# Graph-attention pair stage: normalising four row tiles on ScalarE instead of VectorE

## The reference, cut to what matters

```python
score = s_src + s_dst + einsum(diff, a_dif) + einsum(abs(diff), a_abs) + einsum(hr_src*hr_dst, a_prd)
alpha = leaky_relu(score, negative_slope=0.2)          # one per head and edge: 8 x 10000
ex    = exp(alpha - segment_max(alpha)[src])
att   = ex / (segment_sum(ex, src)[src] + 1e-16)
gnn   = segment_sum(att[:, :, None] * h_e[:, dst], src)
...
x = x + gnn + mix                    # mix: linear attention on the same input
x = x + ffn(_layernorm(x, axis=-1))  # (x - mean) / sqrt(var + 1e-5), over the 512 features
```

## Time and profile before

| | us |
|---|---|
| median of three runs | 1072.98 (1068.33 to 1073.06) |
| the profiled execution, whole | 1073.43 |
| its span, first to last instruction | 1071.6 |
| PE / DVE / ACT / POOL busy in the span | 979.7 / 759.3 / 338.8 / 349.8 |
| TensorE's mean granted clock | 0.967 of 2.4 GHz |

### The profile page before, as it was taken

The page is one execution under the profiler, slowest core; times in us unless marked ns, Lnnn a source line. Parts: engine busy times, 40 slices in busy tenths (PEclk is TensorE's granted clock), DMA queues, the critical chain, the costliest instruction groups (busy, mean ns, idle before and its releaser), DMA issues.

```text
span 1071.6 us, 12287 instructions
## 1 busy us (share of the span) xinstructions
PE 979.7 (91%) x4324; PEld 648.0 (60%) x4324; DVE 759.3 (71%) x1309; ACT 338.8 (32%) x623; POOL 349.8 (33%) x316
## 2 busy tenths in 40 slices
PE   7899999999999979998896899999988859888998
PEld 6874696544494445744454447776666527777864
DVE  8897697343794666845445768998877759999643
ACT  5874473322402213022114122321213304444511
POOL 2006731000300102011010147777777714555500
PEclk9999999999999989999898899999998978999999
DMA  9999120113300114001130244333343287531101
GB/s 308 293 301 293 50 99 1 54 45 117 99 29 1 42 57 146 1 0 56 50 118 0 83 122 122 98 91 100 100 137 93 80 329 292 205 133 56 49 1 48
DMA packets 66093, 115.14 MB, mean 107 GB/s; under 512 B 11517, under 2 KB 43517, under 8 KB 64501
## 3 DMA queue, kind: packets, MB, share of 16 engines
q1 hardware_dynamic: 57077, 93.10, 25.8%
q0 software_dynamic: 8960, 21.31, 7.2%
HBM read 85.91 MB, written 28.49 MB: 107 GB/s over the span
## 4 chain that ended last, share of the span: by engine, by line
PE 40%; DVE 28%; POOL 14%; issue 8%; DMA 7%; ACT 1%; SPq 0%; POOLq 0%; DVEq 0%; ACTq 0%
PE ps L752 16%; PE ps L890 7%; POOL arena L685 6%; DMA pairs<-arena,pairi 5%; DVE arena L1620 5%; POOL pairs L695 4%; DVE arena L1977 4%; PE ps L761 4%; PE ps L795 3%; PE ps L744 3%; DVE arena L1962 2%; DVE arena L1986 2%; PE ps L944 2%; PE ps L1111 2%; POOL small L644 1%
## 5 line engine op out<-in xcount | busy, mean ns | idle before, releaser
L752 PE MATMUL ps<-arena 128*125 128x512 f32 x400 | 180.5, 607 | 1.0 <-DVE xn L1654 1.0
L621 POOL TENSOR_TENSOR small<-small 125x1 f32<-125x1 f32 x50 | 35.0, 699 | 389.8 <-DVE small L1433 389.8
L752 PEld LDWEIGHTS ps<-arena 128*125 128x125 f32 x400 | 75.6, 194 | 91.0 <-issue 89.8
L752 PE MATMUL ps<-arena,xnT 128*125 128x512 f32 x240 | 108.7, 610 | 5.0 <-DVE x L1886 4.2
L1266 ACT ACTIVATE arena<-ps,cols 128x125 f32<-128x125 f32 x120 | 43.2, 466 | 201.9 <-PE ps L744 201.9
L977 PE MATMUL ps<-ex_low,high 125*125 125x512 f32 x400 | 104.2, 406 | 0.0
L695 POOL DMA_INDIRECT pairs<-arena,pairi x80 | 87.2, 1090 | 27.1 <-issue 24.7
L744 PE MATMUL ps<-ident,arena 125*125 125x125 f32 (+3 forms) x425 | 62.4, 283 | 25.9 <-ACT arena L1123 10.0
L719 POOL TENSOR_TENSOR arena<-arena,counts 125x625 f32<-125x625 f32 x40 | 57.5, 1438 | 78.5 <-ACT arena L1387 35.5
L752 PEld LDWEIGHTS ps<-arena,xnT 128*125 128x125 f32 x240 | 46.0, 194 | 60.9 <-issue 59.5
L744 PEld LDWEIGHTS ps<-ident,arena 125*125 125x125 f32 (+3 forms) x425 | 53.5, 168 | 47.7 <-issue 19.4
(11 more groups left out here) (222 smaller groups left out, 1872.1 us busy)
## 6 DMA issues: line engine op xcount, KB each, us to landing
pairs<-fill SPq DMA_DIRECT2D x10, 2500.0 KB, 22.3
arena<-in_mw SPq DMA_DIRECT2D x6, 2048.0 KB, 8.3
arena<-pairs SPq DMA_DIRECT2D x4, 2500.0 KB, 14.2
arena<-pairs SPq DMA_DIRECT2D x8, 1250.0 KB, 6.1
arena<-pairs SPq DMA_DIRECT2D x8, 625.0 KB, 7.6
arena<-in_qkv_w SPq DMA_DIRECT2D x1, 3072.0 KB
arena<-in_cw SPq DMA_DIRECT2D x3, 1024.0 KB, 5.3
arena<-in_w_qkvT SPq DMA_DIRECT2D x1, 3072.0 KB
```

Source lines behind the costliest of these rows:

```text
L752: last = mm(slot[0:m, lo:hi], lhsT_of(k), rhs_of(k)[:, lo:hi], start=(k == 0), stop=(k == ks - 1))
```

## The change

For tiles 0 to 3 the 125x512 instruction leaves DVE. DVE now computes only `shift = -mean * rstd` (125x1, a `scalar_tensor_tensor`) at the same place in its loop and signals a new semaphore `shift_ready`; it waits for `rstd_ready` there, as `ln_apply` did. ACT waits for `shift_ready` and makes the tile as `Identity(rstd * x + shift)`, one 125x512 activation, which then signals `xn_ready`. In ACT's loop this stands in the same step (17, 25, 33, 41) behind the `Exp` and ahead of the four short activations. Tile 4 stays on DVE. `shift` lies in a part of the tile `small` that was free.

```diff
+        shift = small[0:P, 192:192 + NT]
 ...
                     act.activation(Sg, Sg, ACT.Exp, scale=-1.0,
                                    bias=smax[:, 1, h:h + 1]).then_inc(sig("pair_exp"), 1)
+                j, left = divmod(g - LAG - SUM_LAG - NORM_LAG, H)
+                if 0 <= j < NT - 1 and left == H - 1:
+                    act.wait_ge(sig("shift_ready"), j + 1)
+                    act.activation(xn[:, j, :], x[:, j, :], ACT.Identity, scale=rstd[:, j:j + 1],
+                                   bias=shift[:, j:j + 1]).then_inc(sig("xn_ready"), 1)
                 j, h = divmod(g - LAG - SUM_LAG, H)
 ...
                 j, left = divmod(g - LAG - SUM_LAG - NORM_LAG, H)
-                if 0 <= j < NT and left == H - 1:
+                if 0 <= j < NT - 1 and left == H - 1:
+                    lns_done[0] += 1
+                    v.wait_ge(sig("rstd_ready"), lns_done[0])
+                    STT(out=shift[:, j:j + 1], in0=mv[:, j, 0:1], scalar=-1.0, in1=rstd[:, j:j + 1],
+                        op0=ALU.mult, op1=ALU.mult).then_inc(sig("shift_ready"), 1)
+                if j == NT - 1 and left == H - 1:
                     normed_x(j)
```

## The result

| | before | after |
|---|---|---|
| median, us | 1072.97 (1066.86 to 1075.91, 12 runs) | 1080.34 (1074.11 to 1087.19, 12 runs) |
| ratio | | 1.0075, 95% interval 1.0050 to 1.0101 |
| profiled execution / its span | 1073.43 / 1071.6 | 1083.11 / 1081.3 |
| mean granted clock in it | 0.967 | 0.957 |

The changed kernel is slower, by 7.4 us in the median, where 1075.6 was forecast.

The account below looks back on a forecast made before the run. DVE was taken to pace the pair stage for four tiles, PE for the last; -0.56 + 1.34 + 0.47 + 1.4 = +2.65 on 1073.43 gave 1076.08, so 1075.6 us for the median, range 1070.0 to 1079.0.

Parts of the forecast that it names:

- The shift is held: On DVE, the shift ends only with POOL's product, so DVE gains 0.28 us per tile, 0.56 for tiles 0 and 1.
- ScalarE's price: On ACT, the 125x512 activation takes 0.80 us, 0.70 until the next instruction may start.
- The late copies: ACT's copies of exT come 2.07 us late in steps 17 and 25 without loss; step 33 loses 1.34 us.
- The tail: Step 41, at the stage's end: PE's transpose comes later, a loss of 0.47 us, bounds 0 and 0.7.
- TensorE's clock: Behind PE's longer pauses in steps 17 and 25 the clock falls once to 1.2 GHz, costing 1.4 us.
- part 3: The prediction's step on TensorE's clock in steps 17 and 25: one fall expected, 1.4 us.
- Rival (d): Steps 17 and 25: clock low for 12.6 us after a pause, 4.3 us per tile; +9.9, 1082.4; chance 0.08.
- (c): The shift issues ahead of POOL's product and takes 0.16 us; DVE gains 3.1 us; -2.2, 1070.8; chance 0.11.
- (e): PE's delays are won back everywhere and DVE keeps its gain; -0.56, 1072.4; chance 0.07.

Follow-up runs that it names:

- e2: The changed kernel with the shift made by a tensor_scalar with one SBUF input instead of a two-input scalar_tensor_tensor; ratio 1.0015 to the kernel before.
- e5: The changed kernel with POOL's products of steps 16, 24 and 32 starting only when the shift is done; ratio 1.0014 to the kernel before.
- e10: The kernel before, with POOL's products of steps 16, 24 and 32 starting only when VectorE's normalisation of the tile is done; ratio 0.9988.
- e1: The changed kernel with 12, 12 and 7 spare TensorE products filling the pauses of steps 17, 25 and 33; 1074.39 us, ratio 1.0014.
- e8: The changed kernel with only tiles 0 and 1 normalised on ScalarE, the others on VectorE; ratio 1.0057 to the kernel before.
- e7: The changed kernel with only tile 2 normalised on ScalarE, the others on VectorE; ratio 1.0026 to the kernel before.
- e6: The changed kernel with ScalarE's activation cut to 8 of 512 columns, its wait kept; median 1080.27 us, ratio 1.0073 to the kernel before.

## Why the prediction was wrong, point by point

- **The shift is held: right.** 1.46 us were measured where about 1.4 was forecast, ending with POOL's product, and VectorE gained 0.27 us per tile (0.28). Shown by e2 and e5, and by e10 for the instruction that the shift replaces.
- **ScalarE's price: right.** 0.81 us for 0.80.
- **The late copies: right.** TensorE's pauses were 2.94 and 3.16 us, as worked out, and 1.76 in step 33 (a delay of 1.66 on a gap of some 0.1). The tail lost 0.50 (0.47). What all this costs at full clock was put at +1.25; e1 measures 1.5 in the medians and 1.35 in its stage from step 17 on, with +1.33 in step 33 where 1.34 was forecast.
- **TensorE's clock: wrong, and that is the whole error.** The step that failed is part 3. It put the clock at one fall of 1.4 us in the two pauses of steps 17 and 25 and at nothing in step 33, for which it gives no reason. Between e1 and after, which differ in the filled pauses alone, the clock cost 7.4 - 1.5 = 5.9 us in the medians and 11.69 - 1.35 = 10.3 in the profiled executions, with three falls. Two things were mis-sized. First, which pauses count: the two rows of 2.71 us in the earlier trace rows came from an earlier stage, and the prediction took them as the edge between falling and holding. In this stage the clock fell behind pauses of 1.61, 1.67, 1.75, 1.76, 1.82 and 1.89 us, all there were of that length. Second, how long it stays low: 2.7 us up to one step were assumed, 3.4 to 10.5 were measured. The trace of before held a row against both that was not used, a pause of 2.01 us behind which the clock fell and stayed low for 6.7 us (timeline, busy time by stretch):

```profile
610.81 1.09 PE L744 MATMUL ps<-ident,xn 125*128 125x125 f32 x4 [2.01 <-DVE xn L1441]
...
610.80:617.50 6.70, 5.89 (x13) 3.25 (x14) 6.46 (x21) 1.18 (x2) 0.99 (x2) 0.50 0.97 399
```

- **Rival (d) had the mechanism, at 0.08.** It priced 12.6 us at half speed at 4.3 us per tile and found only tiles 0 and 1 in danger; with falls of about 10 us e8 shows 3.1 per tile, and tile 2 adds 4.7 (e7), 1.3 of which the forecast had as lateness. Its time should read 1082.8: 1.25 + 8.6 on 1072.98, not the 1082.4 that stands there. The row that it rested on, 12.6 us at 0.50 with TensorE busy throughout, was the better guide, because it came from this very stage with the same instructions; it was set aside for a row of another stage.
- **The chances.** 0.15 were given to slower by more than 0.5%. The forecast's own reading, that pauses of 0.9 to 1.1 us would grow to 3, should have moved more weight there.
- **(c) and (e)** didn't come: the shift came second in all three steps of the stage, and the delays weren't won back.

What stays open: why the changed kernel's executions spread from 1074 to 1087 us. Their mean granted clocks go along: 0.965 in those of 1074.1 and 1075.9 us, 0.953 in that of 1087.2. So the number and length of falls differ from run to run, but only one execution was profiled, and why a pause of 2.52 us was followed by none (e6) and one of 1.61 by one (e5) isn't known. Nor is why the stage's part ahead of step 17 is up to 1.1 us longer in some executions.

## What to carry to other kernels

Ask of an instruction that moves to another engine not only what it costs there, but whom it stands in front of: 0.8 us on an engine that was idle more than half of the time cost seven, because it and its wait stood ahead of a copy for which TensorE was waiting already, and one step later in the same loop they cost nothing that could be measured. Without the wait the work in that place still cost about five. A long VectorE instruction beside a GpSimd one may be mostly waiting: compare it with the same form elsewhere in the trace before counting its duration as a gain, and note that a tiny replacement can be held just as long. Price a new TensorE pause with the low clock that follows it, and take that from the same stage.

## What the runs showed of the hardware that was not expected

From 930 us on, eleven of the twelve TensorE pauses of 1.61 to 3.16 us in these runs' profiles went along with a fall of the granted clock to 0.50, while those of up to 1.43 us did not. After it had fallen, TensorE worked for 3.4 to 10.5 us at half speed before the clock rose, and the longer stretches did not belong to the longer pauses: 1.67 us was followed by 10.3, and 3.16 by 6.6. Matmuls that nobody reads, put into the pause, kept the clock at 1.00 throughout.
